# One shared-expert group moved into the last attention body: 1, 3 and 4 groups in place of 3 and 5

## The chip, the cores and the metric

The kernel runs on one core of a Trainium2 chip. The metric is the device time of one execution in microseconds (us), lower is better; the median of three executions stands for a kernel.

## What is computed

A gated cross-attention layer over 16 sequences of 224 tokens of width 512 (context 750 tokens, 16 heads of width 32), then a mixture of experts over the 3584 tokens: a shared expert that sees every token, and 16 routed experts of which each token takes two.

```python
h = layernorm(x)
Q, K, V = h@Wq+bq, ctx@Wk+bk, ctx@Wv+bv            # split in 16 heads
attn = softmax((Q@K.T / sqrt(32)) * gate)          # gate: 1 or 0.1 per context token
x = x + tanh(g_xattn) * ((attn@V)@Wo + bo)

h = layernorm(x)
shared = (silu(h@wg_s) * (h@wu_s)) @ wd_s          # 2 shared experts as one of width 512
top2 of softmax(h@router_w), weights normalised
routed = sum over the 2 experts of w * ((silu(h@wg_r[e]) * (h@wu_r[e])) @ wd_r[e])
out = x + tanh(g_ffn) * (shared + routed)
```

## The kernel before, in words

The program is four blocks of engine code one after the other, with a barrier between each two.

**Attention.** `attention_phase` has a setup and then 16 bodies, one for each sequence (`batch` on each engine; bodies 1 to 14 are a hardware loop, the first and the last are written out). A body works on four chunks `c` of four heads. In a chunk TensorE makes 12 score tiles (`score_columns`, tick `u`), ScalarE takes their exponential, GpSimd adds them up (`add_first`, `add_pair`), TensorE multiplies with V (`attend`) and sums (`sum_up`), and VectorE normalises (`normalize_output`). `next_scores` and `maximum` run ahead for later heads: TensorE writes a row of scores into one `score` bank, VectorE takes its maximum, and only then comes the next row. A body but the last also projects Q, K and V of the next sequence in the gaps; `take_proj` rotates these projections over three `proj` banks, in the order of the lists `BODY` and `LAST`. In the last body nothing follows, so those projections are absent. In it SyncE loads the shared expert's weights (`gu_raw`, `d_raw`), and ScalarE (`shared_high`) and VectorE (`shared_low`) split them into a high and a low part. After the last body TensorE still does `attend`, `sum_up`, the output projection (`project_out`), and, after statistics on VectorE, a factor on GpSimd and the normalisation on ScalarE, the transposes (`turn_result`) and the router (`route`). The results go to DRAM as `x1`, `xn_rows`, `xn_cols` and `logits`.

**Head block.** `head_and_slots` works on the first `HEAD` = 3 of the 8 groups of the shared expert (a group is two sequences, 448 tokens, four tiles of 112 rows), and beside them picks the experts and gives each token its slots. A group is 96 matmuls of `gate_up` (4 column blocks `j`, gate and up, 4 chunks `d`, three products of high and low parts) and 48 of `down`. There is one gate bank and one up bank, so the gate product of `j`+1 waits for `silu` of `j`. Group 0 is loaded there (`load_columns`), split by ScalarE (`columns_high`) and GpSimd (`columns_low`). ScalarE also issues four 2 MB loads of the routed experts' weights, behind its first split.

**Routed block.** `routed_experts` runs 72 tiles of 128 slots. The change leaves it as it is.

**Final block.** `shared_and_combine` does the five groups that are left (`HEAVY` = `GROUPS - HEAD`), written out. For each group VectorE splits the hidden values (`hid_s`, `hid_hi`, `hid_lo`), splits the next group's columns (`split_columns`), adds the two routed rows of every token (`total`, eight operations) and then the down banks (four). It also adds routed rows to the groups that the head block had done (`light`: `total_l` and `routed_l`, two operations for each of four tiles). GpSimd fetches routed rows with indirect DMAs of one tile each: 8 for a group, and 8 for a light group. SyncE's queue is in order: the loads of the next group's `total` and of the columns after it stand behind the stores of this group, for which it waits.

These lines set the order of VectorE in the final block before; `light` of group `g - 1` stands between the hidden parts:

```python
for j in range(SC):
    ...
    nc.vector.tensor_tensor(hid_lo[:, j, :], ...).then_inc(parts_ready, 1)
    if 1 <= g <= HEAD:
        light(g - 1, j)
if not last:
    dve.wait_ge(xc_in, 16 * BATCHES * (g + 2))
    split_columns(...)
```

## Time and profile before

| | us |
|---|---|
| median of 3 executions | 2050.35 (2047.47 to 2050.38) |
| the profiled execution, its own time | 2065.15 |
| its span, first to last instruction | 2063.2 |
| head block, first SyncE issue | 1508.04 |
| final block, first matmul | 1890.46 |

The profiled execution is one other than the three timed ones and 14.8 us longer than their median. Starts and durations in the rows are microseconds from the start of its span. Engines are PE (TensorE), DVE (VectorE), ACT (ScalarE), POOL (GpSimd) and SP (SyncE); "SPq" and "ACTq" rows are issues of DMAs. L with a number is a line of the kernel.

### The profile page before, as it was taken

How to read it: one execution, taken by the hardware profiler on the slowest of the kernel's cores; microseconds unless marked ns; L12 is line 12 of the kernel's file. 1: busy time of each engine (PE TensorE's matmuls, PEld its weight loads, DVE VectorE, ACT ScalarE, POOL GpSimd, SP SyncE). 2: the span in 40 equal slices, each digit the busy share in tenths (PEclk: the TensorE clock that was granted, in tenths of full speed). 3: DMA queues.
4: the chain of work that ended last, by engine and by line, in shares of the span. 5: the costliest groups of instructions: out<-in, count | busy, mean ns of one | idle time of the engine just before them, and what ended most of it. 6: DMA issues, size and time to landing. Idle time of an engine off the chain costs nothing. (4 is left out here: it accounts for less than half of the span.)

```text
span 2063.2 us, 40622 instructions
## 1 busy us (share of the span) xinstructions
PE 1948.6 (94%) x12484; PEld 1510.4 (73%) x12485; DVE 1117.1 (54%) x1772; ACT 777.1 (38%) x1541; POOL 1226.6 (59%) x1391
## 2 busy tenths in 40 slices
PE   6799999999999999999999999998769999999899
PEld 5587877878777787877878777785458666666687
DVE  4565565655556555565665656555347333333576
ACT  3335444444544444444444544444222122221000
POOL 2367677776767777677776767766524333333352
PEclk9899999999999999999999999998579999999899
DMA  7754837457383654837557383664062554445675
GB/s 221 187 144 120 240 98 203 137 148 202 107 234 102 183 161 121 246 98 194 143 141 206 109 227 112 173 170 131 19 248 77 179 165 146 149 144 172 178 222 152
DMA packets 170571, 330.51 MB, mean 160 GB/s; under 512 B 20295, under 2 KB 69447, under 8 KB 169879
## 3 DMA queue, kind: packets, MB, share of 16 engines
q1 hardware_dynamic: 156700, 286.97, 49.3%
q0 software_dynamic: 10880, 33.56, 6.0%
q10 hardware_dynamic: 2944, 9.38, 1.2%
q8 instruction: 27, 0.44, 0.1%
q14 instruction: 20, 0.16, 0.0%
HBM read 214.17 MB, written 115.14 MB: 160 GB/s over the span
## 5 line engine op out<-in xcount | busy, mean ns | idle before, releaser
L848 DVE TENSOR_REDUCE neg_max<-score 112x1 f32<-112x750 f32 x512 | 480.7, 939 | 570.4 <-PE score L1129 569.3
L613 ACT ACTIVATE probs_t<-st 125x448 f32<-125x448 f32 x768 | 413.6, 542 | 514.9 <-PE st L1155 512.1
L482 POOL TENSOR_TENSOR acc<-acc,probs_t 125x448 f32<-125x448 f32 x256 | 309.5, 1209 | 66.1 <-ACT probs_t L613 64.3
L1155 PE MATMUL st<-q_stack,k_stack 98*125 98x224 f32 x1536 | 336.1, 302 | 5.0 <-ACT probs_t L613 2.7
L1093 PE MATMUL proj<-ctx_hi,weights 128*128 128x376 f32 (+1 forms) x1024 | 329.7, 347 | 0.0
L1155 PEld LDWEIGHTS st<-q_stack,k_stack 98*125 98x125 f32 x1536 | 269.0, 192 | 60.1 <-issue 28.3
L484 POOL TENSOR_TENSOR acc<-acc,probs_t 125x448 f32<-125x448 f32 x256 | 299.0, 1168 | 20.1
L1129 PE MATMUL score<-k_stack,q_stack 96*112 96x512 f32 (+1 forms) x1024 | 286.1, 361 | 23.8 <-DMA k_stack<-k_parts 12.4
L1103 PE MATMUL proj<-weights,ctx_hi 128*125 128x512 f32 x768 | 249.1, 406 | 5.0 <-issue 5.0
L474 POOL TENSOR_TENSOR acc<-probs_t 125x448 f32<-125x448 f32 x128 | 146.1, 1143 | 168.3 <-PE pv L1181 149.7
L1129 PEld LDWEIGHTS score<-k_stack,q_stack 96*112 96x112 f32 x1024 | 160.5, 179 | 80.7 <-issue 53.5
L1093 PEld LDWEIGHTS proj<-ctx_hi,weights 128*128 128x128 f32 x1024 | 192.4, 190 | 25.3 <-issue 16.1
L1172 PE MATMUL pv<-probs_t,v_sb 125*32 125x224 f32 x3072 | 191.9, 369 | 7.4 <-DVE out_t L871 6.6
L437 POOL TENSOR_TENSOR k_lo<-fresh,k_hi 128x376 fp32r<-128x376 f32 (+1 forms) x128 | 117.1, 915 | 97.3 <-ACT k_hi L583 97.3
L1093 PE MATMUL proj<-parts,weights 128*128 128x376 f32 (+1 forms) x512 | 172.1, 336 | 0.0
L2229 PE MATMUL gu_ps<-gu_sb,xg_t 128*128 x576 | 155.4, 398 | 4.0 <-DVE xg_t L2181 1.7
L2229 PEld LDWEIGHTS gu_ps<-gu_sb,xg_t 128*128 128x128 f32 x576 | 99.0, 191 | 78.4 <-issue 66.4
L1103 PE MATMUL proj<-weights,parts 128*125 128x512 f32 x384 | 152.5, 397 | 0.0
L1103 PEld LDWEIGHTS proj<-weights,ctx_hi 128*125 128x125 f32 x768 | 125.7, 189 | 34.6 <-issue 16.1
L1081 PE MATMUL proj<-xn_t,wq_sb 128*128 128x224 f32 x512 | 122.3, 364 | 12.4 <-DVE q_lo L831 10.3
L1116 PE MATMUL proj<-wo_sb,out_t 128*112 128x512 f32 x256 | 126.0, 607 | 0.0
L1172 PEld LDWEIGHTS pv<-probs_t,v_sb 125*32 125x32 f32 x3072 | 82.8, 111 | 55.9 <-DVE out_t L871 10.0
(212 smaller groups left out, 2758.3 us busy)
## 6 DMA issues: line engine op xcount, KB each, us to landing
k_stack<-k_parts SPq DMA_DIRECT2D x192, 375.0 KB, 6.2
ctx_raw<-in_ctx_t SPq DMA_DIRECT2D x64, 375.0 KB, 10.0
k_parts<-k_hi SPq DMA_DIRECT2D x64, 375.0 KB, 6.9
k_parts<-k_lo SPq DMA_DIRECT2D x64, 375.0 KB, 7.2
y_slots<-y_sb SPq DMA_DIRECT2D x72, 256.0 KB, 3.0
q_stack<-q_parts SPq DMA_DIRECT2D x64, 224.0 KB, 5.9
gu_sb<-in_w_gu ACTq DMA_DIRECT2D x4, 2048.0 KB, 15.6
x_in<-in_x SPq DMA_DIRECT2D x16, 448.0 KB, 9.2
```

Of the source, the lines that this page charges most:

```text
L474: nc.gpsimd.tensor_tensor(acc[0:KW, 2 * pair:2 * pair + 2, :], tiles(c, 0, pair, 0), tiles(c, 0, pair, 1), ALU.add).then_inc(added, 1)
L482: nc.gpsimd.tensor_tensor(both, both, tiles(c, p, pair, 0), ALU.add).then_inc(half_added, 1)
L484: nc.gpsimd.tensor_tensor(both, both, tiles(c, p, pair, 1), ALU.add).then_inc(added, 1)
L613: act.activation(probs_t[0:KW, (c * PHASES + p) % 2, u % HC, :], st[u % 2][0:KW, 0:2 * L], ACT.Exp)\
L848: nc.vector.tensor_reduce(neg_max[:, h // HC % 2, h % HC, t:t + 1], score[0:QW, 0:S], axis=AX.X, op=ALU.max, negate=True).then_inc(maxed, 1)
L1093: ins = nc.tensor.matmul(bank[:, 0:w], wp[:, d, c * P:(c + 1) * P], xp[:, d, at:at + w], start=(d == 0 and k == 0), stop=(d == DC - 1 and ...
L1103: ins = nc.tensor.matmul(bank[0:KW, :], xp[:, d, kt * KW:(kt + 1) * KW], wp[:, d, :], start=(d == 0 and k == 0), stop=(d == DC - 1 and k = ...
L1116: ins = nc.tensor.matmul(bank[0:QW, :], out_t[:, c, t * QW:(t + 1) * QW], wo_sb[:, c, :], start=(c == 0), stop=(c == DC - 1))
L1129: ins = nc.tensor.matmul(score[0:QW, at:at + w], q_stack[0:ROWS, h, t * QW:(t + 1) * QW], k_stack[0:ROWS, h, at:at + w], start=True, stop= ...
L1155: ins = nc.tensor.matmul(st[u % 2][0:KW, k * L:(k + 1) * L], k_stack[0:SHIFTED, h, kt * KW:(kt + 1) * KW], q_stack[0:SHIFTED, h, :], start ...
L1172: ins = nc.tensor.matmul(pv[j * DH:(j + 1) * DH, 0:L], v_sb[0:KW, kt, at:at + DH], probs_t[0:KW, (c * PHASES + p) % 2, j, k * L:(k + 1) * ...
L2229: ins = nc.tensor.matmul(gu_ps[k % 2][:, 0:GATE_UP], xg_t[:, k % 2, c, :], gu_sb[:, bass.ds(expert, 1), c, :].rearrange("p a m -> p (a m)" ...
```

## The change

The last attention body also computes group 0 of the shared expert. Its columns are loaded early in that body; `product` does its gate and up products in 28 pieces between the score tiles of chunks 1 to 3, on the three `proj` banks, and ScalarE copies each result out. After the body come silu, the hidden parts and `down` in four portions, into the banks of the scores; the sum is stored over `x1`. ScalarE and VectorE also split the columns of group 1 there, into the tiles that the head block uses. The splits of the shared weights come one at a time between the maxima, where they came in a row. The head block has three groups still, 1 to 3, and starts with the columns of its first one split; `columns_low` of group 0 and its loads are gone, and the four weight loads are ScalarE's first issues there. The final block has four groups. Each of them also has one light group: all eight `light` operations stand in one run behind `split_columns` and ahead of `total`. Two buffers (`RING`) hold the light groups where three were, and the load of a light group stands ahead of the next `total` and columns in SyncE's queue.

```diff
-LAST = ("V4", "V5", "O0", "SH1", "O1", "SH2", "SH3", "YT0", "YT1", "LG")
+LAST = ("V4", "V5", "O0", "SH1", "O1", "G0", "SH2", "U0", "G1", "U1", "SH3", "G2", "YT0", "YT1", "LG", "U2", "G3", "U3")
...
+            def product(name, steps):
+                bank = take_proj(B - 1, name) if steps[0] == 0 else proj[bank_of(B - 1, name)]
...
+                for d in range(*steps):
+                    if name == "G0":
+                        pe.wait_ge(columns_lo, d + 1)
+                        pe.wait_ge(shared_lo, d + 1)
+                    for n, (wp, part) in enumerate((("gu_hi", 0), ("gu_hi", 1), ("gu_lo", 0))):
+                        ins = nc.tensor.matmul(bank[:, 0:GTOK], shared[wp][:, d, at:at + P], xc_parts[:, part, d, :],
...
             attend(B - 1, 3, 2)
             sum_up(B - 1, 3)
+            down(0)
             for t in range(QT):
                 project_out(B - 1, t, B, (0, 4))
+            for j in (1, 2):
+                down(j)
             for t in range(QT):
                 turn_result(B - 1, t, B)
+            down(3)
             for t in range(QT):
                 route(t, B)
...
+            copy_product("U3", 3, up_sb)
+            silu(0)
+            silu(1)
+            hidden_high(0)
+            silu(2)
+            silu(3)
+            for j in range(1, SC):
+                hidden_high(j)
+            for d in range(DC):
+                columns_high(1, d)
             act.wait_ge(x1_stored, B * 16)
             for t in range(QT):
                 normalize(x_res, t, xn2_ready, 2 * B - 1)
...
-HEAD = 3
+HEAD = 4
+FIRST_IN_BLOCK = 1
...
-            for d in range(DC):
-                columns_high(0, d)
             for n in range(LOADS):
...
+                if s == 0:
+                    sp.wait_ge(total_stored, 16 * GT * (HEAD - FIRST_IN_BLOCK))
+                    for l in range(RING):
+                        load_light(l)
+                sp.wait_ge(light_done, s + 1)
...
                 if not last:
+                    if s + RING < HEAD:
+                        sp.wait_ge(light_stored, 16 * (s + 1))
+                        load_light(s + RING)
                     sp.wait_ge(out_stored, 16 * (GT * s + GT))
                     load_total(s + 1)
...
-                    if 1 <= g <= HEAD:
-                        light(g - 1, j)
                 if not last:
                     dve.wait_ge(xc_in, 16 * BATCHES * (g + 2))
                     split_columns(nc, dve, xc, xc_parts, chain4, base + links[0], xc_ready)
                     links[0] += DC
+                for t in range(GT):
+                    light(g, t)
                 dve.wait_ge(total_in, 16 * g + 16)
```

Where instructions now stand, at three places. First TensorE in the fourth chunk of the last attention body and behind it (`st` are score tiles, `pv` with `v_sb` is `attend`, `pv` with `acc` is `sum_up`, `proj` with `wo_sb` is the output projection). Before:

```order
L1172 MATMUL pv<-probs_t,v_sb 32x224 x8
L1155 MATMUL st<-q_stack,k_stack 125x224 x6
L1172 MATMUL pv<-probs_t,v_sb 32x224 x8
L1155 MATMUL st<-q_stack,k_stack 125x224 x2
L1172 MATMUL pv<-probs_t,v_sb 32x224 x8
L1181 MATMUL pv<-acc,ones_col 32x224 x4
L1116 MATMUL proj<-wo_sb,out_t 112x512 x8
```

After, the same place:

```order
L1305 MATMUL proj<-xc_parts,weights 128x448 x3
L1273 MATMUL st<-q_stack,k_stack 125x224 x2
L1290 MATMUL pv<-probs_t,v_sb 32x224 x8
L1305 MATMUL proj<-xc_parts,weights 128x448 x3
L1273 MATMUL st<-q_stack,k_stack 125x224 x2
L1305 MATMUL proj<-xc_parts,weights 128x448 x6
L1290 MATMUL pv<-probs_t,v_sb 32x224 x8
L1327 MATMUL pv<-acc,ones_col 32x224 x4
L1318 MATMUL st<-sd_hi,hid_hi_l 112x512
L1318 MATMUL st<-parts,hid_hi_l 112x512
L1318 MATMUL st<-sd_hi,hid_lo_l 112x512
```

Products of three or six matmuls stand between the score tiles, and twelve matmuls of `down` (the first three are shown) stand between `sum_up` and the output projection.

Second VectorE in the final block, within one middle group. Before (the second half of a group's hidden parts up to its down banks):

```order
L2444 TENSOR_TENSOR hid_lo<-hid_s,hid_hi 128x448
L2425 SCALAR_TENSOR_TENSOR total_l<-routed_l,weight,total_l 112x512
L2428 SCALAR_TENSOR_TENSOR total_l<-routed_l,weight,total_l 112x512
L2048 CAST xc_parts<-xc 128x448 x2
L2051 TENSOR_TENSOR xc_parts<-xc,xc_parts 128x448
L2048 CAST xc_parts<-xc 128x448
L2051 TENSOR_TENSOR xc_parts<-xc,xc_parts 128x448
L2048 CAST xc_parts<-xc 128x448
L2051 TENSOR_TENSOR xc_parts<-xc,xc_parts 128x448 x2
L2456 SCALAR_TENSOR_TENSOR total<-routed,weight,total 112x512 x8
L2466 SCALAR_TENSOR_TENSOR total<-down_bank,tanh_g,total 112x512 x4
```

After, from the last row of `split_columns`:

```order
L2247 TENSOR_TENSOR xc_parts<-xc,xc_parts 128x448 x2
L2629 SCALAR_TENSOR_TENSOR total_l<-routed_l,weight,total_l 112x512
L2632 SCALAR_TENSOR_TENSOR total_l<-routed_l,weight,total_l 112x512
L2629 SCALAR_TENSOR_TENSOR total_l<-routed_l,weight,total_l 112x512
L2632 SCALAR_TENSOR_TENSOR total_l<-routed_l,weight,total_l 112x512
L2629 SCALAR_TENSOR_TENSOR total_l<-routed_l,weight,total_l 112x512
L2632 SCALAR_TENSOR_TENSOR total_l<-routed_l,weight,total_l 112x512
L2629 SCALAR_TENSOR_TENSOR total_l<-routed_l,weight,total_l 112x512
L2632 SCALAR_TENSOR_TENSOR total_l<-routed_l,weight,total_l 112x512
L2660 SCALAR_TENSOR_TENSOR total<-routed,weight,total 112x512 x8
L2670 SCALAR_TENSOR_TENSOR total<-down_bank,tanh_g,total 112x512 x4
```

The eight light operations moved from between the hidden parts to between the column split and `total`.

Third SyncE's queue in the final block, between two groups. Before:

```order
L2355 DMA out<-total_l 112x4x512
L2360 DMA out<-total 112x512 x4
L2338 DMA total<-x 112x4x512
L2038 DMA xc<-xn_cols 128x4x224 x2
L2350 DMA total_l<-x 112x4x512
```

After:

```order
L2553 DMA out<-total_l 112x4x512
L2558 DMA out<-total 112x512 x4
L2539 DMA total_l<-x 112x4x512
L2535 DMA total<-x 112x4x512
L2234 DMA xc<-xn_cols 128x4x224 x2
```

The light group's load moved from behind the columns to ahead of them.

## Rows read from the trace of the kernel before

**Rows 1.** The page: engines' busy time and share; granted clock in 40 slices.

```profile
PE 1948.6 (94%) x12484; PEld 1510.4 (73%) x12485; DVE 1117.1 (54%) x1772; ACT 777.1 (38%) x1541; POOL 1226.6 (59%) x1391
...
PEclk9899999999999999999999999998579999999899
```

**Rows 2.** Chain that ended last, final block: start, us, what.

```profile
1902.84 12.22 another core or an unknown queue
...
1937.00 10.02 another core or an unknown queue
...
1955.69 11.16 PE down_bank L2489 x48
1966.84 2.44 PE gate_bank L2480 x12
```

**Rows 3.** Five-microsecond windows, attention's end: length, PE, PEld, DVE, ACT, POOL, clock, DMA.

```profile
1475.00:1480.00 5.00, 4.22 (x27) 2.44 (x24) 2.45 (x1) 2.05 (x4) 4.92 (x4) 0.50 0.00 0
...
1485.00:1490.00 5.00, 5.00 (x10) 1.90 (x7) 2.24 (x3) 0.00 (x0) 0.00 (x0) 0.54 0.00 0
1490.00:1495.00 5.00, 4.52 (x11) 1.59 (x9) 1.12 (x2) 0.00 (x0) 0.00 (x0) 1.00 0.00 0
```

**Rows 4.** Timeline, last attention body and behind: start, duration, instruction, [idle before].

```profile
1439.87 5.98 POOL L484 TENSOR_TENSOR acc<-acc,probs_t 125x448 f32<-125x448 f32 x1
1440.25 4.62 DVE L822 TENSOR_TENSOR weights<-shared_raw,weights 128x1024 fp32r<-128x1024 f32 x4
1445.78 0.97 PE L1129 MATMUL score<-k_stack,q_stack 96*112 96x512 f32 x2 [4.01 <-DVE neg_max L848]
...
1484.30 0.97 PE L1181 MATMUL pv<-acc,ones_col 125*32 125x224 f32 x8 [2.51 <-POOL acc L484]
1485.20 9.31 PE L1116 MATMUL proj<-wo_sb,out_t 128*112 128x512 f32 x16
1500.03 1.52 ACT L602 ACTIVATE x_res<-x_res,neg_mean,rstd 112x512 f32<-112x512 f32 x2 [20.02 <-POOL neg_mean L455]
```

**Rows 5.** Timeline, start of the head block.

```profile
1508.04 0.34 SPq L1663 DMA_DIRECT2D logit<-logits  x1
1512.45 0.69 DVE L1860 TENSOR_REDUCE top<-logit 112x32 f32<-112x512 f32 x1 [6.32 <-DMA logit<-logits]
1517.86 2.61 PE L1976 MATMUL gate_bank_h<-xc_parts,weights 128*128 128x448 f32 x6 [11.96 <-POOL xc_parts L1689]
1518.10 0.61 ACT L1772 ACTIVATE probs<-probs 112x512 f32<-112x512 f32 x1
1518.73 1.28 ACT L1749 ACT_TABLE_LOAD   x1
1527.61 2.62 PE L1976 MATMUL gate_bank_h<-xc_parts,weights 128*128 128x448 f32 x12
```

**Rows 6.** Timeline, final block: DMA issues, gathers of one run, VectorE's work.

```profile
1918.40 0.69 DVE L2048 CAST xc_parts<-xc 128x448 fp32r<-128x448 f32 x2
...
1921.75 5.51 DVE L2456 SCALAR_TENSOR_TENSOR total<-routed,weight,total 112x512 f32<-112x512 f32 x8
...
1929.92 0.94 SPq L2360 DMA_DIRECT2D out<-total  x1
...
1973.45 0.75 DVE L2425 SCALAR_TENSOR_TENSOR total_l<-routed_l,weight,total_l 112x512 f32<-112x512 f32 x1
...
1968.41 2.29 SPq L2360 DMA_DIRECT2D out<-total  x4
1976.15 0.34 SPq L2338 DMA_DIRECT2D total<-x  x1
...
1986.99 0.93 POOL L2377 DMA_INDIRECT routed_l<-y_slots,slot_i  x1 [0.30 <-issue]
...
1993.53 0.70 DVE L2048 CAST xc_parts<-xc 128x448 fp32r<-128x448 f32 x2 [0.21 <-DMA xc<-xn_cols]
...
2022.29 0.70 DVE L2048 CAST xc_parts<-xc 128x448 fp32r<-128x448 f32 x2 [1.99 <-DMA xc<-xn_cols]
```

More of the change, by code:

```diff
@@ L1030, in _ @@
             links[0] = 0
+            hidden(0)
+            hidden_low(0)
             normalize_output(B - 1, 3, base)
+            for j in range(1, SC):
+                hidden(j)
+                hidden_low(j)
             for t in range(QT):
@@ L1313, in batch @@
                 next_scores(b, 12, 0)
+                if last:
+                    product("G0", (0, 1))
                 if not last:
@@ L1317, in batch @@
                 attend(b, 1, 0)
+                if last:
+                    product("G0", (1, 2))
                 if not last:
@@ L1324, in batch @@
                 score_columns(b, 1, 8)
+                if last:
+                    product("G0", (2, 3))
                 if not last:
@@ L1329, in batch @@
                 next_scores(b, 13, 0)
+                if last:
+                    product("G0", (3, 4))
                 if not last:
@@ L1333, in batch @@
                 attend(b, 1, 1)
+                if last:
+                    product("U0", (0, 1))
                 if not last:
@@ L1337, in batch @@
                 score_columns(b, 1, 11)
+                if last:
+                    product("U0", (1, 2))
                 if not last:
@@ L1343, in batch @@
                 next_scores(b, 14, 0)
+                if last:
+                    product("U0", (2, 3))
                 if not last:
@@ L1346, in batch @@
                 score_columns(b, 2, 1)
+                if last:
+                    product("U0", (3, 4))
                 if not last:
@@ L1350, in batch @@
                 score_columns(b, 2, 2)
+                if last:
+                    product("G1", (0, 1))
                 if not last:
@@ L1356, in batch @@
                 next_scores(b, 15, 0)
+                if last:
+                    product("G1", (1, 2))
                 if not last:
@@ L1360, in batch @@
                 score_columns(b, 2, 4)
+                if last:
+                    product("G1", (2, 3))
                 if not last:
@@ L1366, in batch @@
                 score_columns(b, 2, 5)
+                if last:
+                    product("G1", (3, 4))
                 if not last:
@@ L1371, in batch @@
                 next_scores(b, 16, 0)
+                if last:
+                    product("U1", (0, 1))
                 if not last:
@@ L1375, in batch @@
                 attend(b, 2, 0)
+                if last:
+                    product("U1", (1, 2))
                 if not last:
@@ L1379, in batch @@
                 score_columns(b, 2, 8)
+                if last:
+                    product("U1", (2, 3))
                 if not last:
@@ L1386, in batch @@
                 next_scores(b, 17, 0)
+                if last:
+                    product("U1", (3, 4))
                 if not last:
@@ L1390, in batch @@
                 attend(b, 2, 1)
+                if last:
+                    product("G2", (0, 1))
                 if not last:
@@ L1394, in batch @@
                 score_columns(b, 2, 11)
+                if last:
+                    product("G2", (1, 2))
                 if not last:
@@ L1401, in batch @@
                 next_scores(b, 18, 0)
+                if last:
+                    product("G2", (2, 3))
                 if not last:
@@ L1419, in batch @@
                     route(1, b)
+                if last:
+                    product("U2", (0, 2))
                 if not last:
@@ L1425, in batch @@
                 score_columns(b, 3, 5)
+                if last:
+                    product("U2", (2, 4))
                 if not last:
@@ L1430, in batch @@
                 next_scores(b, 20, 0)
+                if last:
+                    product("G3", (0, 1))
                 if not last:
@@ L1434, in batch @@
                 attend(b, 3, 0)
+                if last:
+                    product("G3", (1, 2))
                 if not last:
@@ L1440, in batch @@
                 score_columns(b, 3, 8)
+                if last:
+                    product("G3", (2, 4))
                 if not last:
@@ L1445, in batch @@
                 next_scores(b, 21, 0)
+                if last:
+                    product("U3", (0, 1))
                 if not last:
@@ L1449, in batch @@
                 attend(b, 3, 1)
+                if last:
+                    product("U3", (1, 2))
                 if not last:
@@ L1646, in head_and_slots @@
         CONSTS = 15
+        IN_BLOCK = HEAD - FIRST_IN_BLOCK
         def chunk_of(ap, n):
@@ L1707, in _ @@
             iota(token_row[:, :], [[0, 1]], step=1)
-            for d in range(2, DC):
-                columns_low(0, d)
             for i in range(2):
```

283 lines of the change are left out of this document (196 added, 87 removed).

## The prediction

> **What bounds the kernel now.** I read the page first. PE is busy 94% of the span, and its granted clock is 0.98 to 1 in most slices but falls to 0.8, 0.5 and 0.7 where attention ends and the head block starts [rows 1]. So a group of the shared expert costs most where PE is full at full clock, and least in that dip. Next comes the chain of waits, which names what ends last: in the final block it is PE's own products, `gate_bank` 2.44 us for each j and the 48 matmuls of `down` 11.16 us [rows 2]. A group there is 4 x (2.44 + 2.44) + 11.16 = 30.7 us of PE, with `up` taken as `gate`. The block lasts from 1890.46 to the end, 172.7 us, and 5 x 30.7 = 153.4 of it is PE's work; ahead of the second and third group the chain has two stretches of 12.22 and 10.02 us that it puts to an unknown queue [rows 2]. Third, the windows at the end of attention show PE at half clock (0.50) with gaps until 1485, and back at 1.00 in the window from 1490, behind one window in which PE was busy all 5.00 us [rows 3]. Last, the timelines of the three places that the change touches [rows 4 to 6].
>
> **Last attention body.** It gains 96 matmuls. One costs 2.44 / 12 = 0.203 us at full clock, so 19.5 us together; at half clock 39. They go into some 60 us of chunks 1 to 3. At 1475 the window has 4.22 of 5 us busy at clock 0.50 [rows 3]: the same work at full clock is 2.1, so 2.9 of 5 us are free there, and 60 us hold some 35 us, if the clock is full. With the new work PE is full in these chunks even at half clock (4.22 + 5 x 39/60 = 7.5 of 5), which is the state after which the clock came back [rows 3]. I take it that it comes back here and that the body keeps the pace of its maxima and sums. Four splits in a row cost VectorE 4.62 us now; beside them one sum of GpSimd takes 5.98 us and PE waits 4.01 us for the maximum [rows 4]. Spread one by one, that wait goes in part; `columns_low` adds four subtractions early in chunk 1, some 0.6 each (a `xc_parts` split of eight operations takes 3.4 in the final block, 1921.75 - 1918.40 [rows 6]). I take -1.5 us for the time of `sum_up`, which waits for GpSimd at 1484.30 now, with a range of -5 to +8.
>
> The row of 5.98 us shows two engines held by each other. The Trainium skill (SBUF — State Buffer, "SBUF: two separate sides") says that a VectorE operation with two inputs in SBUF and a GpSimd operation take a shared pair of ports as an exclusive lock, each for its whole instruction. The trace agrees: the sum ends after the last of the four splits. By that rule spread splits delay each sum by one split (1.15 us) and not by four; it is in my -1.5 and changes no chance.
>
> **Behind the body.** PE meets `down(0)`, 12 matmuls: 2.44 us at full clock, 5 at half, and it needs the first hidden part: copy, silu with its table (1.28 [rows 5]) and four operations of 0.6, some 4.7 us behind the last exponential. `sum_up` waits for GpSimd in that time anyway. The output projection behind it took 9.31 us, half of it at half clock [rows 3, 4]; 4.8 of them lie ahead of 1490, so 2.4 are saved if the clock is full. `down(1)` and `down(2)` stand where PE waits for the statistics (ScalarE's idle time there is 20.02 us [rows 4]): nothing. `down(3)` adds 2.5 us ahead of the router. Four stores of `total` stand ahead of the columns' and logits' stores in SyncE's queue, four issues of 0.5 us: 2. Together the head block starts 5 - 2.4 + 2.5 + 2 - 1.5 = +5.6 us if nothing covers them, 0 with all cover kept; I take +2, 1510 in place of 1508.04.
>
> **Head block.** From its first issue to the second gate product are 1527.61 - 1508.04 = 19.6 us now: the first product waits for `columns_low` of GpSimd until 1517.86, 11.96 us [rows 5]. After, the first products start at once, and the second gate product waits only for ScalarE's first silu, which stands behind the logits' exponential. That is: logits landed 4.4 us after the issue (1512.45), and 1.5 more since 8 MB of weights are now asked for at once; maximum 0.69 and subtraction, 1.4; exponential 0.61; table 1.28; silu 0.54: 9.8, and 1.5 for a PE that runs at half clock: 11.3. The gain is 8.2, less the 2 us of the later start: **-6** (range -9 to 0). Behind it PE is dense until the final block, so the gain goes through; the routed block is as before.
>
> The table load stands 0.02 us behind the exponential [rows 5]. The Trainium skill (ScalarE: Activation LUTs, "What ACT_TABLE_LOAD costs") gives 1.28 us for the load, as here, and 1.38 more for draining the engine. By the row the change's two further switches cost 2.6 us beside other work; by the page 5.3, and the head block's gain would be 1.4 smaller.
>
> **Final block.** One group less is -30.7 us if PE stays the bound. I think that it does not, because of what now stands in a row. Call E the end of the issue of a group's four stores: 1929.92 + 0.94 = 1930.86, then 1968.41 + 2.29 = 1970.70 [rows 6]. SyncE waits for these stores: the next `total` is issued at 1976.15, 5.45 us after E, the columns behind it, and they have landed at 1993.53, E + 22.8. The group after the next has landed its columns at 2022.29, 11.64 us after its `total` was asked for at 2010.65 and some 17 after its E: there GpSimd has 8 gathers in flight; with 16 they go on to 1986.99 + 0.93, E + 17.2 [rows 6]. After the change every group has 16 gathers, and the light load (0.9 MB) stands ahead of `total` and columns. The parts: columns landed E + 24 (between 22.8 as now and 26.1 for a queue that ends with the light load's end), split 3.4, eight light operations of 0.77 = 6.2 (0.75 and the step to the next), `total` 5.51, four bank additions and the last store's issue 3.3 (1930.86 - 1927.26 = 3.6 with the first of these groups) [rows 6]: a cycle of 42.4 us, against 30.7 of PE's work. In before the light operations lie between the hidden parts, where VectorE waits for PE; now they lie between split and `total`, on the cycle. PE waits for the split columns and then, at its third gate product, for `hid_s`, which VectorE reaches only behind the banks.
>
> The first E came 1930.86 - 1890.46 = 40.4 us after the block's first matmul, and with the light run ahead of it 46.6. Two cycles: 84.8. The last group: 16 gathers end at E + 17.2, the last landed 2 later, 19.2; light 6.2, `total` 5.5, banks 2.8, stores 3.2 to their landing: 36.9. Sum 46.6 + 84.8 + 36.9 = 168.3 us for 172.7: **-4**, not -30.7 (range -20 to +4).
>
> **Sum.** -6 - 4 = -10: the profiled execution 2055 us, and 2050.35 - 10 = **2040** for the median. The 14.8 us between the two are not explained by the trace; if the stretches of 12.22 and 10.02 are absent from timed runs, before is shorter there and the change has up to 7 us less to gain.
>
> **Rivals.** A, the above: 2040, chance 0.50. B, **the columns land as with 8 gathers**, 17 us after E; the cycle is then 17 + 3.4 + 6.2 + 5.5 + 3.3 = 35.4, two of them save 14 more, and 2 us in the last group: 2024, chance 0.20. For it: the gathers are small and there are more gaps; against: both 16-gather groups took 22 us and more. The full -30.7 would need columns landed within 13 us, and no row has that. C, **slower: the last body keeps half clock.** The new matmuls then take 0.41 us each, 78 of them in the 40 us of chunks 2 and 3 that are busy for 40 x 4.22/5 = 34 now [rows 3]: 32 - 6 = +26 us, with the -10 at 2066. It decides if half clock holds over more than about half of that stretch; against it stands the window from 1490. Chance 0.08. D, **it gains nothing**: the head block's gain is eaten by the later start, the columns take 26.1, which adds 4 in two cycles, and the first 12.22 us stretch grows by 2: 2050, chance 0.22.
>
> **How the numbers follow.** A measurement of this kernel tells some 0.2%, 4.1 us, from no change: bounds 2046.25 and 2054.45. A spreads from 2030 to 2052: 0.46 faster, 0.03 same, 0.01 slower. B is faster, 0.20. C is slower, 0.08. D: 0.17 same, 0.05 slower. Together 0.66, 0.20, 0.14. The range 2022 to 2058 leaves out C and B's lower end.
>
> **What would show it.** Granted clock near 1.00 in the last body's chunks 2 and 3, and `sum_up` near 1483. The head block's first issue near 1510 and its second gate product some 11 us later. In the final block: `xc_parts` waiting for the DMA of `xc`, one run of eight light operations behind each split, `total` loads some 42 us apart, PE's third gate product waiting for `hid_s`, and a length of 168 us. Wrong it would be if PE has no waits in that block (then 2010 to 2015), or if the maxima of the last body wait for PE at half clock.

## The result, and the profile after

The changed kernel took 2060.20 us (median of 4, 2059.44 to 2064.09), the kernel before in the same comparison 2050.06 (median of 4, 2047.47 to 2050.38): ratio 1.0062, 95% interval 1.0042 to 1.0082. It is 10 us slower where 10 us less was forecast, and outside the range (2022 to 2058). Two later comparisons of the same two kernels gave 1.0023 (1.0008 to 1.0037) and 1.0061 (1.0040 to 1.0082): slower each time.

The profile says something else at first sight: the span after is 2057.9 us, 5.3 less than the 2063.2 of before. The profiled execution of before (2065.15 us) was itself 15 us above its median, that of after (2059.64) within 1 us of its own, so the profiled pair shows -5.5 us where the medians show +10. The page of after (busy time of each engine; granted clock in 40 slices):

```profile
PE 1935.6 (94%) x12484; PEld 1503.5 (73%) x12485; DVE 1110.8 (54%) x1768; ACT 787.4 (38%) x1559; POOL 1216.8 (59%) x1385
...
PEclk9899999999999999999999999999989999999987
```

The dip of the clock at the end of attention has become shallower (one slice at 0.8 where three stood at 0.8, 0.5 and 0.7 [rows 1]), and a new one stands in the last two slices. Both come from one place each, as the stages show. I cut every profile at the same seven instructions: the store of `x1` early in the last body, `sum_up` at its end, the next store of `x1`, the head block's first load, its second gate product, the first tile of the routed block, the final block's first matmul, the end.

| stage, us | before | after | before (3rd) | after (3rd) |
|---|---|---|---|---|
| last body | 61.6 | 67.0 | 59.1 | 67.2 |
| to the store of x1 | 11.2 | 14.2 | 11.4 | 14.2 |
| to the head block's first load | 12.6 | 18.3 | 12.6 | 18.2 |
| to its second gate product | 19.6 | 7.5 | 18.0 | 7.5 |
| to the routed block | 98.5 | 98.9 | 98.4 | 99.8 |
| routed block | 264.3 | 264.1 | 263.3 | 264.0 |
| final block | 172.7 | 166.8 | 166.5 | 167.4 |

The two columns on the right are profiles that were taken on one chip (`before_third`, `after_third`), those on the left the first ones. In the first pair the first three stages, the end of attention, cost 14.1 us, the start of the head block gives 12.1 back, the routed block is the same, and the final block, which was to bring the gain, brings 5.9 in one pair and costs 0.9 in the other.

**The last body.** TensorE's `sum_up` of each of its chunks in the changed kernel, in order of time:

```profile
1404.57 0.56 PE L1327 MATMUL pv<-acc,ones_col 125*32 125x224 f32 x8
...
1425.29 0.56 PE L1327 MATMUL pv<-acc,ones_col 125*32 125x224 f32 x8
...
1455.22 0.56 PE L1327 MATMUL pv<-acc,ones_col 125*32 125x224 f32 x8
...
1471.83 0.56 PE L1327 MATMUL pv<-acc,ones_col 125*32 125x224 f32 x8
...
1488.25 0.59 PE L1327 MATMUL pv<-acc,ones_col 125*32 125x224 f32 x8 [1.89 <-POOL acc L517]
```

and in the kernel before:

```profile
1425.23 0.56 PE L1181 MATMUL pv<-acc,ones_col 125*32 125x224 f32 x8
...
1448.99 0.97 PE L1181 MATMUL pv<-acc,ones_col 125*32 125x224 f32 x8
...
1467.68 0.97 PE L1181 MATMUL pv<-acc,ones_col 125*32 125x224 f32 x8
```

The second distance is 29.9 us after and 23.8 before; the next two are 16.6 and 16.4 after, 18.7 and 16.6 before [rows 4]. The loss is in one chunk. TensorE's timeline of that chunk names it:

```profile
1433.23 1.46 PE L1305 MATMUL proj<-xc_parts,weights 128*128 128x448 f32 x3 [2.55 <-DVE weights L900]
...
1441.04 0.85 PE L1305 MATMUL proj<-xc_parts,weights 128*128 128x448 f32 x3 [1.65 <-DVE weights L900]
...
1444.70 1.46 PE L1305 MATMUL proj<-xc_parts,weights 128*128 128x448 f32 x3 [2.25 <-DVE weights L900]
```

Three pieces of the first gate product (`G0`) wait 6.45 us for the weights that VectorE is only then splitting, and the scores, whose maxima VectorE waits for, are behind them in TensorE's queue. The windows of the same profile (length, PE, PEld, DVE, ACT, POOL, clock, DMA) show the clock that rival C was about:

```profile
1435.00:1450.00 15.00, 11.09 (x60) 7.51 (x59) 4.48 (x6) 3.83 (x7) 5.12 (x4) 0.62 0.11 33
1450.00:1465.00 15.00, 13.66 (x107) 10.98 (x105) 7.50 (x10) 8.10 (x17) 9.07 (x8) 1.00 0.23 70
1465.00:1480.00 15.00, 14.85 (x133) 12.05 (x133) 4.97 (x8) 8.35 (x17) 10.54 (x9) 1.00 0.21 65
```

It is at full speed (1.00, 2.4 GHz) from 1450 on, where it was 0.50 before: that step was right for chunks 2 and 3. In the window from 1435, where the waits are, it is 0.62.

**Behind the body and in the head block**, timeline of after over several engines:

```profile
1494.43 7.03 PE L1234 MATMUL proj<-wo_sb,out_t 128*112 128x512 f32 x16
...
1504.27 2.61 POOL L479 TENSOR_TENSOR rstd<-var_eps,minus_half 112x2 f32<-112x2 f32 x1 [16.07 <-DVE var_eps L865]
...
1515.31 1.65 PE L1184 MATMUL proj<-rw_sb,xn_t 128*112 128x16 f32 x16
...
1520.75 0.32 SPq L1869 DMA_DIRECT2D logit<-logits  x1
...
1524.24 0.69 DVE L2057 TENSOR_REDUCE top<-logit 112x32 f32<-112x512 f32 x1 [7.06 <-DMA logit<-logits]
...
1528.23 2.72 PE L2172 MATMUL gate_bank_h<-xc_parts,weights 128*128 128x448 f32 x12 [0.50 <-ACT silu_h L1950]
```

The output projection starts 6.2 us behind `sum_up` in place of 0.9 (`down(0)` stands between), and takes 7.03 in place of 9.31 [rows 4]. GpSimd's first operation on the statistics takes 2.61 us, and the router's matmuls start 5.5 us behind the transposes (1509.84), 1.8 before, since `down(3)` stands between. So the head block starts 12.7 us later than before [rows 5]. From there the second gate product is 7.5 us away in place of 19.6; the logits landed 3.5 us after their load.

**Final block**, SyncE's queue and VectorE in the second and the last group:

```profile
1931.49 2.29 SPq L2558 DMA_DIRECT2D out<-total  x4
1933.82 1.26 SPq L2539 DMA_DIRECT2D total_l<-x  x1
1939.31 0.34 SPq L2535 DMA_DIRECT2D total<-x  x1
1939.70 1.28 SPq L2234 DMA_DIRECT2D xc<-xn_cols  x2
...
1959.85 0.69 DVE L2244 CAST xc_parts<-xc 128x448 fp32r<-128x448 f32 x2 [12.40 <-DMA xc<-xn_cols]
...
1961.22 4.26 PE L2684 MATMUL gate_bank<-xc_parts,weights 128*128 128x448 f32 x12 [4.52 <-DVE xc_parts L2247]
...
1975.20 2.29 SPq L2558 DMA_DIRECT2D out<-total  x4
...
1977.73 4.72 PE L2684 MATMUL gate_bank<-xc_parts,weights 128*128 128x448 f32 x12 [4.90 <-DVE hid_s L2643]
...
2018.81 2.29 SPq L2558 DMA_DIRECT2D out<-total  x4
...
2040.65 0.75 DVE L2629 SCALAR_TENSOR_TENSOR total_l<-routed_l,weight,total_l 112x512 f32<-112x512 f32 x1 [5.08 <-DMA routed_l<-y_slots,slot_i]
```

The stores stand 43.7 and 43.6 us apart; the columns land 26.1 us behind the stores' end (1959.85 - 1933.78), VectorE waits 12.40 us for them, and TensorE waits twice, 4.52 us for their split and 4.90 for `hid_s`, which VectorE reaches only behind the down banks. That is the cycle of the forecast (42.4). The clock's dip in the last slices goes with these waits: at 1961.22 and 1977.73 twelve matmuls take 4.26 and 4.72 us, where they take 2.44 at full clock [rows 2].

### The profile page after: what moved, and what is told of

Read it like the earlier page. It is cut to its first block and busy times, and to the rows that moved or that the text cites. A ratio compares the mean times of both kernels' runs of the same rounds, so it can differ in the third digit from the quotient of the medians.

```text
span 2057.9 us, 40619 instructions
## 1 busy us (share of the span) xinstructions
PE 1935.6 (94%) x12484; PEld 1503.5 (73%) x12485; DVE 1110.8 (54%) x1768; ACT 787.4 (38%) x1559; POOL 1216.8 (59%) x1385
## 5 line engine op out<-in xcount | busy, mean ns | idle before, releaser
L1273 PE MATMUL st<-q_stack,k_stack 98*125 98x224 f32 x1536 | 330.3, 297 | 3.1 <-DMA q_stack<-shift_rows 1.9
L1247 PE MATMUL score<-k_stack,q_stack 96*112 96x512 f32 (+1 forms) x1024 | 284.9, 360 | 20.1 <-DMA k_stack<-k_parts 11.9
L1290 PE MATMUL pv<-probs_t,v_sb 125*32 125x224 f32 x3072 | 186.7, 361 | 4.4 <-DVE out_t L963 4.2
```

What stands on the lines that cost most here:

```text
L1247: ins = nc.tensor.matmul(score[0:QW, at:at + w], q_stack[0:ROWS, h, t * QW:(t + 1) * QW], k_stack[0:ROWS, h, at:at + w], start=True, stop= ...
L1273: ins = nc.tensor.matmul(st[u % 2][0:KW, k * L:(k + 1) * L], k_stack[0:SHIFTED, h, kt * KW:(kt + 1) * KW], q_stack[0:SHIFTED, h, :], start ...
L1290: ins = nc.tensor.matmul(pv[j * DH:(j + 1) * DH, 0:L], v_sb[0:KW, kt, at:at + DH], probs_t[0:KW, (c * PHASES + p) % 2, j, k * L:(k + 1) * ...
```

## Experiments: the final block

Twelve runs on three chips and four more on one; ratios are to the kernel before in the same comparison. First, what the times of before are worth. `before_again` is the kernel before, unchanged. "Stretches" are waits of TensorE, ScalarE and VectorE that the profile puts to no engine of this core; its view of waits calls them "remote".

> The kernel before, unchanged, with a new profile. Theory 1, the stretches that the first profile put to an unknown queue (12.22 and 10.02 us) belong for the most part to that one execution: own time near 2050 us, final block (first matmul to end) 156 to 160 us in place of 172.7. Theory 2, they are there in every execution: the final block is 172 to 173 us and the 15 us that the profiled run was longer lie in attention or in the routed block.

Measured 2057.55 us, final block 170.5. Theory 1 falls (the block is 170.5 us and not 156 to 160), and theory 2 misses its 172 by 1.5: there are such stretches again (TensorE's `up_bank` matmuls come singly with up to 1.06 us between them, ScalarE 40.0 us in 5 waits that the view of waits puts to "remote"). But the kernel before itself took 2057.57 us in the median of this comparison (2048.22 to 2061.65), not 2050.

> The changed kernel; in the final block the columns of the group after the next are asked for as soon as the split has freed their tile, ahead of the stores of the group and not behind them. Theory 1, the columns' way (store, wait, total, columns: landed 26 us behind the last store's issue) sets the cycle of 43.6 us: the split starts behind the hidden parts, the gathers of the light rows become the last wait (landed 19 us behind the stores), the cycle falls to about 34 and the time by 2 x 9.5 = 19 to about 2041 us. Theory 2, the DMA engines are what is short and the columns only show it: the columns land early but gathers and total later, under 8 us gained, 2052 to 2060.

```diff
-                if not last:
-                    sp.wait_ge(xc_ready, DC * s + DC)
-                    load_columns(sp, xc, xn_cols, HEAD + s + 1, xc_in)
+                if s == 0:
+                    sp.wait_ge(xc_ready, DC)
+                    load_columns(sp, xc, xn_cols, HEAD + 1, xc_in)
...
+                if s + 2 < HEAVY:
+                    sp.wait_ge(xc_ready, DC * (s + 2))
+                    load_columns(sp, xc, xn_cols, HEAD + s + 2, xc_in)
                 sp.wait_ge(light_done, s + 1)
```

Measured 2049.34 us (ratio 0.9969, 0.9950 to 0.9987), final block 158.5. VectorE waits no more for columns; the stores' issues in the profile stand 38.1 us apart:

```profile
1930.82 2.29 SPq L2561 DMA_DIRECT2D out<-total  x4
...
1968.93 2.29 SPq L2561 DMA_DIRECT2D out<-total  x4
...
2006.92 2.29 SPq L2561 DMA_DIRECT2D out<-total  x4
```

Theory 1 holds in kind: 5.6 us of a cycle are the columns' way, 8.3 us of the block (166.8 in the changed kernel's first profile). The 9.5 a cycle that it named did not come. This profile has stretches (VectorE 36.5 us in four) and that of the 166.8 has none, so the edit may be worth more; how much isn't shown.

> The changed kernel; light operations go back between the hidden parts of the next group (the last group has two light groups, one there and one ahead of total), and the light load goes back behind the columns. Theory 1, light stands on the cycle (6.2 us a group, and 3.3 us of waiting for the first light gathers) and its load ahead of the columns costs 3 us: cycle 34.8, first store 9.5 us earlier, together 27 us less, 2033 us. Theory 2, only the columns' way counts and the light operations slide into its waits: the light load's 3 us twice, 2053 us.

```diff
                         .then_inc(parts_ready, 1)
+                    if g:
+                        light(g - 1, j)
...
-                for t in range(GT):
+                for t in range(GT if last else 0):
                     light(g, t)
```

and in SyncE's queue the light load stands behind the columns again. Measured 2043.11 us (0.9921, 0.9897 to 0.9946), final block 152.7, cycles of 37.4 and 33.6. Theory 1 in kind: the light operations and the light load's place, which this run changes together, cost the cycle 6 to 10 us; of the 27 us that it named, 14.1 came in the block.

> The changed kernel with both edits: columns asked for ahead of the stores, light between the hidden parts of the next group. Theory 1, PE is the bound of a cycle again (30.7 us): first stores' end 33 us behind the block's first matmul, two cycles of 31, last group 37 (its 16 gathers and light are unchanged): 132 us in place of 166.8, 2025 us. Theory 2, gathers and DMA set it: cycles of 36 or more, above 2035 us.

Both edits. Measured 2036.89 us (0.9908, 0.9883 to 0.9933), final block 144.5, cycles of 34.4 and 28.5. Neither theory is met whole: the cycles are under 36, but the time is above 2035. Against 166.8 the two edits add (8.3 and 14.1, 22.3 together); against 171.4, the block of the changed kernel in a profile with stretches (`after_again`, below), they take 12.9 and 18.7, and 26.9 together. Each takes a part of the same 43.7. Against 132 expected, 12.5 are missing: some 9 before the first stores (1929.54 - 1887.98 = 41.6 us for 33), where there are stretches again.

> The kernel before, with the columns asked for ahead of the stores as in the run cols_early. Theory 1, the final block before is bound by TensorE and by stretches in which engines wait for no engine; the columns cost it under 5 us (waits of 0.21 and 1.99 us for them): same, within 3 us. Theory 2, columns and stores behind each other cost it as much as the changed kernel (8 us and more): 2045 us or less, and then the edit and not the changed kernel is what the run both gained by.

The same edit of the columns in the kernel before (on another chip). Measured 2041.61 us against 2046.06 (0.9984, 0.9966 to 1.0002): 4 us less in the medians, and by the interval 0 to 7, so less than the 8 that theory 2 asked for. The edit is worth more to the changed kernel, and a part of what `cols_early` and `both` gained is to be had without the change. The final block took 157.7 us, and TensorE waited for nothing there but its start; five groups of 30.7 are 153.4. So without late columns and without stretches the block before takes 158, not 172.7.

> The kernel before with a third profile, on one chip with the runs above. Theory 1, final block 170 to 173 us with two stretches in which VectorE waits for no engine, if its own time is above 2050, and 158 to 162 without them if it is below. Theory 2, its final block is 170 us whatever its time.

Measured 2050.36 us (a single execution; before's median in this comparison is 2045.03), final block 166.5, no wait that is put to "remote". Its waits for columns there (engine, line, waited for: us, times, longest):

```profile
DVE xc_parts L2048 <- DMA xc<-xn_cols: 15.0, 3, 10.5
...
PE gate_bank L2480 <- DVE xc_parts L2051: 4.0, 1, 4.0
```

and those of the changed kernel on the same chip (`after_third`):

```profile
DVE xc_parts L2244 <- DMA xc<-xn_cols: 25.8, 2, 13.2
...
PE gate_bank L2684 <- DVE hid_s L2643: 10.7, 3, 5.0
PE gate_bank L2684 <- DVE xc_parts L2247: 10.0, 2, 5.3
```

Neither theory is met as written: time and block lie between them. TensorE waits 4.0 us in one place before, and 20.7 us in five after: 10.0 for split columns and 10.7 for `hid_s`.

> The changed kernel, unchanged, beside new runs of the kernel before, whose times ran from 2048 to 2062 us in the last comparison and from 2047 to 2050 in the first. Theory 1, the change costs some 10 us whatever the runs of before do: ratio near 1.005. Theory 2, the kernel before has stretches in which engines wait for no other engine (12.22 and 10.02 us in its first profile, 9 to 12 in its second) in a varying number of its executions, and the first comparison met few of them: ratio 0.999 to 1.003, with the changed kernel itself again at 2057 to 2064.

Measured 2062.45 us (1.0023, 1.0008 to 1.0037), before at 2057.3. Theory 2 is right about the ratio. On this chip the changed kernel has the stretches too (final block 171.4):

```profile
DVE hid_s L2643 <- remote: 44.0, 5, 10.2
ACT silu_s L2609 <- remote: 37.3, 5, 12.9
```

Here VectorE waits 11.9 us for columns where it waits 25.8 in `after_third`, and the block is only 4.0 us longer than there: the changed kernel has waits in which such stretches can pass, and before, with TensorE as its bound, has few. That this is why the ratio is smaller here is argued, not shown.

> The changed kernel, on one chip with the next run. The times of before differ between comparisons (medians 2050, 2057 and 2046 us), and the ratio of the changed kernel with them (1.0062, 1.0023). Theory 1, in executions of before without the stretches that wait for no engine its final block takes 158 us (run before_cols: 157.7) and the changed kernel's takes 167: the ratio is near 1.005 where before is fast and near 1.002 where it is slow; here 6 us above the next run. Theory 2, the difference is between chips and the ratio here is again 1.002 with the next run at the same time as this.

Measured 2056.93 us (1.0061, 1.0040 to 1.0082), before at 2045.03. Theory 1, also in the 6.6 us above the single execution of `before_third`: where before takes 2045 or 2050 us the change costs 12 and 10 us, where it takes 2057 it costs 5.

> The kernel before; the eight gathers of the light rows in each of the first three groups of the final block wait for the hidden parts of that group, two for each. Theory 1, the stretches in which TensorE, ScalarE and VectorE wait for no engine (22.2 us in the first profile's final block) come from instructions that are late behind 16 gathers in a row: they shrink, the final block falls to 158 to 163 us, and the time is 5 to 10 us less than before's and varies less. Theory 2, they are not bound to the gathers: final block and spread of times as in before.

```diff
                     for t in range(GT):
+                        pool.wait_ge(parts_ready, SC * s + t + 1)
                         for k in range(TOP):
                             gather(routed_l[:, s, t, k, :], s, k, t, light_got[s])
```

Measured 2046.10 us (1.0001, 0.9988 to 1.0015), 2037.91 to 2050.49: no gain and no smaller spread in the times, as theory 2 has it, though the profiled execution had a final block of 157.9 (166.5 in `before_third`). The chip of this comparison showed no such stretch in any profile, so the cause of the stretches isn't settled by it.

> As best2, and in the final block's first group the eight gathers of the light rows wait for the hidden parts, two for each, in place of following the eight others at once. In every profile but the changed kernel's own, TensorE, ScalarE and VectorE have stretches in that group in which they wait for no engine, 7 to 15 us in all, while 16 gathers and 2.7 MB of loads are under way. Theory 1, the instructions themselves come over the same DMA engines and are late behind the gathers: with fewer gathers at once the stretches shrink, 3 to 8 us less than best2. Theory 2, they have nothing to do with the gathers: same as best2, or slower by the later light rows.

The same edit, in the first group only, on top of `best2` (below). Measured 2020.77 us against 2020.96: the same. Neither profile had a stretch to take away.

## Experiments: the end of attention

> The changed kernel; the four pieces of the first gate product move from the middle of chunk 1 to its end (two and two, where the first up product began, which moves to the start of chunk 2). In the changed kernel these pieces wait 2.55, 1.65 and 2.25 us for the split of the weights, with the scores behind them in TensorE's queue, and chunk 1 lasts 29.9 us (23.8 before). Theory 1, these waits make the last body longer: chunk 1 falls to 24 or 25 us, the last body (store of x1 to sum_up) from 67 to 61 to 63, time 4 to 6 us less. Theory 2, VectorE's added work and the half clock make it longer, and the waits only fill time: chunk 1 stays above 28 us.

```diff
-LAST = ("V4", "V5", "O0", "SH1", "O1", "G0", "SH2", "U0", "G1", "U1", "SH3", "G2", "YT0", "YT1", "LG", "U2", "G3", "U3")
+LAST = ("V4", "V5", "O0", "SH1", "O1", "SH2", "G0", "U0", "G1", "U1", "SH3", "G2", "YT0", "YT1", "LG", "U2", "G3", "U3")
...
-                    product("U0", (0, 1))
+                    product("G0", (0, 2))
...
-                    product("U0", (1, 2))
+                    product("G0", (2, 4))
```

(the four single pieces of `G0` are gone, `U0` follows in two pieces in chunk 2). Measured 2051.68 us (1.0025, 1.0006 to 1.0043). `sum_up` of chunks 0 and 1:

```profile
1422.47 0.97 PE L1327 MATMUL pv<-acc,ones_col 125*32 125x224 f32 x8
...
1445.44 0.56 PE L1327 MATMUL pv<-acc,ones_col 125*32 125x224 f32 x8
```

23.0 us in place of 29.9, the body 61.1 in place of 67.0: theory 1. The place of the pieces was the loss. It is more than their 6.45 us of waiting: without the waits TensorE is busy all of 1435 to 1450, and its granted clock is 0.92 there, 0.62 in the changed kernel. What the waits cost and what the lower clock behind them cost isn't separated. The time is 5.2 us below that of the changed kernel on this chip (2056.93, `after_third`).

> The run g0_late on one chip with the changed kernel. Its last body was 61.1 us long in the profile, against 67.0 to 68.6 in six profiles with the gate product in its old place. Theory 1, the 6 us come through to the end: 5 to 7 us less than after_third. Theory 2, they are given back behind the body (the transposes and stores took 18.8 against 18.3, nothing else moved): under 3 us less.

Measured 2053.85 us (1.0041, 1.0028 to 1.0053), 3.1 less than `after_third` (2056.93). The body is 61.2 us again. The routed block began 6.7 us earlier (1616.24 for 1622.94), and the final block took 170.1 us in place of 167.4: between the theories. The 6 us reach the final block, which took from 166.6 to 170.1 us in three profiles on this chip; 4.6 us are left at the end of the profiles and 3.1 in the medians.

> The changed kernel with only the low parts of the second group's columns moved from behind the statistics to behind the copy of the logits. Theory 1, VectorE's four subtractions hold GpSimd's first operation of the statistics (2.61 us, 0.70 in the kernel before): it takes 0.70 again and the normalisation starts 1.9 us earlier after the statistics (4.86 us from var_eps to x_res in the changed kernel, 2.95 in the one before). Theory 2, the 2.61 us come from something else (the trace's GpSimd spans are rough): 4.8 us remain.

```diff
             result_statistics(B, 2 * B - 1, base)
-            for d in range(DC):
-                columns_low(1, d)
...
             copy_logits(B, B - 1)
+            for d in range(DC):
+                columns_low(1, d)
```

A single execution took 2051.57 us. That is 11 us below the median of `after_again`, but 4.8 of it lie ahead of the last body and 2.7 in the routed block, which the edit doesn't touch; the effect is read from the stage. GpSimd's operation:

```profile
1495.74 0.70 POOL L479 TENSOR_TENSOR rstd<-var_eps,minus_half 112x2 f32<-112x2 f32 x1 [14.52 <-DVE var_eps L865]
```

0.70 in place of 2.61, and from the store of `x1` to the head block 16.2 in place of 18.3 us: theory 1. The Trainium skill (SBUF — State Buffer, "SBUF: two separate sides") has the rule: a VectorE operation with two inputs in SBUF and a GpSimd operation that reads SBUF exclude each other for a whole instruction. The trace agrees: in the changed kernel VectorE's four subtractions run from 1504.09 to 1506.31 and GpSimd's operation from 1504.27 to 1506.88. The forecast had cited it for the splits in the body and missed the place where the change put four subtractions beside the statistics.

> The changed kernel; behind the last attention body the output projection comes ahead of all of down, all four portions of down stand between the projection and the transposes, and the low parts of the second group's columns come behind the copy of the logits. Theory 1, the head block starts 12.7 us later than before because of five terms: sum_up 4.0, down(0) ahead of the projection 5.3 less 2.3 of clock, the power on GpSimd beside columns_low 1.9, down(3) ahead of the router 3.7 less 1.5, stores 1.7. The edit removes the second, the fourth and the fifth but lengthens the wait ahead of the transposes by some 3: head block's first issue near 1513 in place of 1520.75, time 7 us less. Theory 2, the start of the head block is not on the path (its second gate product waits for something that does not move): 0.

```diff
-            down(0)
             for t in range(QT):
                 project_out(B - 1, t, B, (0, 4))
-            for j in (1, 2):
+            for j in range(SC):
                 down(j)
             for t in range(QT):
                 turn_result(B - 1, t, B)
-            down(3)
```

with the edit of `low_last`. Measured 2058.70 us (1.0013, 0.9997 to 1.0028), 4 less than `after_again` on the same chip, between the theories. The head block's first load is 25.3 us behind `sum_up` in place of 32.5, as theory 1 has it, but the second gate product is then 10.6 us away and not 7.5:

```profile
1516.11 0.69 DVE L2055 TENSOR_REDUCE top<-logit 112x32 f32<-112x512 f32 x1 [7.05 <-DMA logit<-logits]
...
1520.10 4.26 PE L2170 MATMUL gate_bank_h<-xc_parts,weights 128*128 128x448 f32 x12 [3.46 <-ACT silu_h L1948]
```

The logits land 6.6 us after their load (1509.51), and TensorE waits 3.46 us for the silu that stands behind their exponential. Four 2 MB weight loads are under way beside them, but so they are in the changed kernel, where the logits land after 3.5; why they are later here isn't shown. What the tail gains, the logits take in part (3.1 us), and the way to the routed block 2.5 more (101.3 for 98.8).

> The changed kernel with the edits of the runs both and tail together. The final block's gain (22 us in the profile of both) and the tail's 7 are in different places: sum 29 from the changed kernel, 2029 to 2031 us. Rival, they are not additive since the head start is hidden: 2037 as in both.

Both and tail together: 2036.67 us (0.9900, 0.9875 to 0.9925), no less than `both`: the rival's time. The 7 us of the tail are there (25.7 us from `sum_up` to the head block's first load, 32.6 in `both`), but the logits landed 9.2 us after their load here, the second gate product is 13.1 us away for 8.1, and the final block takes 150.4 us for 144.5. The gain is not hidden but given back behind it.

> The changed kernel with the final block of both, the low parts moved as in low_last, the gate product moved as in g0_late, and the four 2 MB weight loads behind the exponential of the logits instead of ahead of it (the logits then land 3.5 to 4.5 us after their load, in place of 3.5 to 9). Sum of the single effects from both's 2036.9: low parts 2, gate product 5, logits 1: 2029 us. Rival, the body's 5 us do not add (TensorE's clock falls again in chunks 1 and 2): 2034.

```diff
-            for n in range(LOADS):
...
             act.wait_ge(shifted, 1)
             act.activation(probs2[:, :, :], probs2[:, :, :], ACT.Exp).then_inc(exped2, 1)
+            for n in range(LOADS):
...
```

with both, low_last and g0_late. Measured 2020.96 us against 2046.06 (0.9864, 0.9832 to 0.9896): 1.4% faster than before, with `spread` the fastest of all. The ratio is 0.0044 below that of `both`, 9 us for the 8 of the sum; the intervals are too wide to tell the sum from its rival, but the body of 61.2 us (68.6 in `both`) speaks for the sum. Against before with the columns' edit alone (`before_cols`, 2041.61) it is 1.0% faster. Head block's start to the second gate product 8.1, final block 138.6 us, with cycles of 32.2 and 30.7, the second of them TensorE's own work alone:

```profile
1914.54 2.29 SPq L2557 DMA_DIRECT2D out<-total  x4
...
1946.73 2.29 SPq L2557 DMA_DIRECT2D out<-total  x4
...
1977.41 2.29 SPq L2557 DMA_DIRECT2D out<-total  x4
```

With TensorE as the bound again, the group that the change moved brings 19.1 of its 30.7 us: four groups take 138.6 us here, five took 157.7 in `before_cols`. One cycle of 30.7 is gone, but from the end of the last cycle's stores to the end it takes 40.7 us here and 30.9 there, since this last group has 16 gathers and two light groups.

## Why the prediction was wrong

**Final block: the working was right, the block it was set against was not.** It forecast 168.3 us from the first matmul and 166.8 were measured: first stores' end 42.6 us in (46.6 forecast), cycles of 43.7 and 43.6 (42.4), columns landed at 26.1, the upper bound (24 taken), last group 36.8 (36.9). The step that failed is "168.3 us for 172.7: -4", taken from a profiled execution and subtracted from a median 14.8 us below it. In the profiled pair this term and the whole come out near the forecast (-5.9 for -4, -5.5 for -10); the rest of the 20 us lies between that execution and the median. The text saw the risk and put it at 7 us. On the chip without stretches the pair of unchanged kernels gives +0.9 (166.5 and 167.4); against the 157.9 of `before_spread`, whose edit only holds gathers back, it is +9.5. So there the term is +1 to +10, not -4. That the timed executions of the first comparison had short blocks too is argued from their times; no profile of one was taken.

**Last body: -1.5 forecast, +5.4 measured** (+8.1 in the pair on one chip), at the upper end of its -5 to +8. The step "I take it that the body keeps the pace of its maxima and sums" failed. It weighed the clock and the time that is free on TensorE, and in chunks 2 and 3 both were as it said: their 16.6 and 16.4 us are no longer than before's 18.7 and 16.6. It did not ask what the first piece waits for: the change both spreads the splits (one between two maxima) and has `G0` wait for each, in a queue where scores stand behind it. `g0_late` gives those 6 us back (61.1, 61.2 us of body, and 61.2 in both kernels built on it).

**Behind the body: +2 forecast for the head block's start, +12.7 measured**; 4.0 of it are `sum_up`'s. The term of `down(0)` was right (5.3) and the projection's saving too (2.3 for 2.4), but the sum was set to +2, for cover that wasn't there: 5.6, its own value "if nothing covers them", was the one to take. Missing were 1.9 us of GpSimd behind the subtractions and 1.2 of `down(3)` (3.7 for 2.5); the router's matmuls gave 1.5 back, and the stores took 1.7 for 2.

**Head block: the gain was larger than forecast**, 12.1 us from start to second gate product for 8.2. The mechanism, a wait for the silu behind the logits' exponential, is the one forecast; two terms were mis-sized. The logits landed after 3.5 us, not 5.9 (in `tail` and `best` they took 6.6 and 9.2), and the 1.5 us added for half clock were not on the chain: 9.8 less 2.4 is 7.4, and 7.5 were measured. The 1.38 us of draining that the prediction weighed for a table load did not show either: the load follows the exponential by 0.02 us, and the silu the load by 0.01. Net of the later start it is +0.7 at the final block's first matmul for -6; 1.4 us of that execution's lead at the last body are in it.

**Rivals.** C (half clock stays) did not come. D had the right parts, gain eaten by the later start and columns at 26.1, with too small a price; even its own parts add to 2052 and not 2050. No rival was about a new wait in TensorE's queue.

## What to carry to other kernels

A piece of work that is put in gaps of an in-order queue must have its inputs ready when its turn comes: ask for each piece what it waits for and what stands behind it, before asking whether the engine has time. A load whose buffer is free early should not stand in a queue behind stores that are waited for; moved ahead of them it was worth 8.3 us of the changed kernel's final block, and in the kernel before 4 us, which its interval doesn't set apart from none. If the profiled execution is longer than the timed ones by more than the effect, find where it is longer before setting a sum against a stage of it.

## What had not been expected

The kernel before took 2057 us in the median on two chips and 2045 to 2046 on a third, with the same code. On the first two every profile has stretches in the final block, 5 to 15 us in which ScalarE, VectorE and TensorE wait for no engine ("remote", or matmuls one by one 1.0 us apart), while 16 gathers are under way; on the third, in eight profiles, none. In the first comparison the profile of before has them and that of after has none. That instructions themselves arrive late behind the gathers would fit, and was not shown.

The routed block, the same in all kernels, took from 261.7 to 266.7 us in 18 profiles. So the spans of two profiles can differ by 5 us by this block alone; cut at the same instructions, the other stages can still be compared.
